# Narrow attention of the third layer: scores on row halves, values as stationary blocks on column strips, outputs divided after the sums

## The reference

```python
B, LQ, D, H, HD, LK = 4, 256, 256, 16, 16, 64
x = layer_norm(hidden_states, ln1_w, ln1_b)
q = (x @ q_w + q_b).reshape(B, LQ, H, HD).transpose(0, 2, 1, 3)
k = (encoder_hidden_states @ k_w + k_b).reshape(B, LK, H, HD).transpose(0, 2, 1, 3)
v = (encoder_hidden_states @ v_w + v_b).reshape(B, LK, H, HD).transpose(0, 2, 1, 3)
scores = jnp.einsum('bhqd,bhkd->bhqk', q, k) / 4
scores = jnp.where(mask, scores, finfo.min)
attn = jax.nn.softmax(scores, axis=-1)
out = jnp.einsum('bhqk,bhkd->bhqd', attn, v).transpose(0, 2, 1, 3).reshape(B, LQ, D)
hidden = out @ cproj_w + cproj_b + residual
```

## Time and profile before

| what | before |
| --- | --- |
| median of 3 runs | 957.06 us |
| lowest, highest | 953.86, 961.48 us |
| span of the profiled execution | 957.6 us |
| PE busy | 881.7 us (92%), 5624 matmul records |
| DVE, ACT, POOL busy | 604.0, 491.8, 484.3 us |
| chain that ended last | PE 70%, DVE 19%, issue 5%, POOL 3% |
| attention 2, first turn to MLP 2's second block | 529.4 to 616.7 us |

### The profile page before, as it was taken

One profiled execution on the slowest core, in us unless ns is written; L12 is line 12 of the kernel. 1 busy time (PEld: TensorE's weight loads), 2 busy tenths in 40 slices (PEclk: granted clock), 3 DMA queues, 4 the chain that ended last, 5 costly groups with the idle time before them and its releaser, 6 DMA issues.

```text
span 957.6 us, 15739 instructions
## 1 busy us (share of the span) xinstructions
PE 881.7 (92%) x5624; PEld 737.2 (77%) x5624; DVE 604.0 (63%) x1344; ACT 491.8 (51%) x1205; POOL 484.3 (51%) x507
## 2 busy tenths in 40 slices
PE   4889876899999999999899898899999999999898
PEld 3677755899966789666797787899975689757788
DVE  3688887416779757796423545325779867798440
ACT  2566655654753356533663332764763347632662
POOL 2667876474543345465293170184544335465383
PEclk8699999999999999999999988999999999999999
DMA  6823312002550025200002000101570015200001
GB/s 188 294 91 87 102 38 96 5 2 72 168 213 1 1 70 162 100 1 0 23 2 88 1 2 0 64 37 40 160 254 0 1 35 164 67 1 1 1 12 34
DMA packets 26673, 64.04 MB, mean 67 GB/s; under 512 B 2995, under 2 KB 15843, under 8 KB 25444
## 3 DMA queue, kind: packets, MB, share of 16 engines
q1 hardware_dynamic: 26596, 63.03, 20.2%
HBM read 57.22 MB, written 5.77 MB: 66 GB/s over the span
## 4 chain that ended last, share of the span: by engine, by line
PE 70%; DVE 19%; issue 5%; POOL 3%; ACT 1%; DMA 1%; SPq 1%; DVEq 0%; POOLq 0%
PE ps L964 7%; PE ps L904 6%; PE ps L863 6%; PE ps L865 6%; PE ps L893 5%; PE ps L940 4%; PE ps L762 3%; PE ps L705 3%; PE ps L706 3%; PE ps L707 3%; PE ps L686 3%; DVE prob L1658 3%; PE ps L687 3%; PE ps L688 3%; DVE mx L1657 3%
## 5 line engine op out<-in xcount | busy, mean ns | idle before, releaser
L964 PE MATMUL ps<-arena,pT_all 128*128 128x256 f32 x512 | 116.6, 381 | 5.7 <-DVE x L1678 3.6
L964 PEld LDWEIGHTS ps<-arena,pT_all 128*128 128x128 f32 x512 | 96.2, 190 | 32.3 <-issue 15.1
L940 PE MATMUL ps<-arena,hT 128*128 128x512 f32 x256 | 115.5, 594 | 0.0
L536 POOL TENSOR_TENSOR rstd<-var,neg_half 128x1 f32<-128x1 f32 (+1 forms) x56 | 33.9, 606 | 155.1 <-DVE var L1487 155.1
L543 POOL TENSOR_TENSOR arena<-arena,rinv 128x640 f32<-128x640 f32 x64 | 80.4, 1257 | 55.4 <-DVE rinv L1472 55.3
L570 POOL TENSOR_TENSOR prob<-prob,rinv 128x512 f32<-128x512 f32 x32 | 49.5, 1547 | 113.2 <-DVE rinv L1671 113.2
L1196 ACT ACTIVATE arena<-ps,nb 128x320 f32<-128x320 f32 x128 | 66.4, 523 | 58.1 <-DVE nb L1458 57.9
L1239 ACT ACTIVATE arena_r<-ps,cols 128x256 fp32r<-128x256 f32 x128 | 66.5, 520 | 55.1 <-PE ps L688 55.0
L512 POOL TENSOR_TENSOR vacc<-vacc,vpart 128x256 f32<-128x256 f32 x60 | 44.0, 734 | 98.6 <-ACT vpart L1311 98.3
L589 POOL TENSOR_TENSOR arena_r<-arena,arena_r 128x512 fp32r<-128x512 f32 x64 | 83.9, 1333 | 13.2 <-ACT arena L1240 13.2
L686 PE MATMUL ps<-hH,w1H 128*128 128x256 f32 x256 | 75.2, 294 | 11.9 <-DVE prob L1658 5.1
(11 more groups left out here) (164 smaller groups left out, 2350.9 us busy)
## 6 DMA issues: line engine op xcount, KB each, us to landing
ring<-in_heads_dram SPq DMA_DIRECT2D x64, 512.5 KB, 3.6
w<-in_w_dram SPq DMA_DIRECT2D x8, 1024.0 KB, 7.3
first_r<-spare_k SPq DMA_DIRECT2D x24, 160.0 KB
first_q<-spare_q SPq DMA_DIRECT2D x48, 64.0 KB, 2.6
spare_k<-HL SPq DMA_DIRECT2D x8, 320.0 KB, 2.4
spare_q<-HL SPq DMA_DIRECT2D x8, 256.0 KB, 2.3
x<-in_x_dram SPq DMA_DIRECT2D x1, 1024.0 KB, 6.0
lnb<-in_lnb_dram SPq DMA_DIRECT2D x4, 256.0 KB, 6.6
```

What stands on the lines that cost most here:

```text
L940: last = mm(ps[:, SCORES[k][half], :], hT[:, k, d, 0:P], A[:, d, b // 2, cols_of, sl, :].rearrange("p r s k -> p r (s k)"), start=(d == 0) ...
L964: last = mm(ps[:, 6, 0:D], pT[:, k, c, :], VW[:, b, c, :], start=(c == 0), stop=(c == PAIRS - 1))
```

## The change

The scores of a group of four heads are now two matmuls, each with half of the rows (64: two heads) and 128 columns, into banks 0 and 1; KC is half as wide. The values are now the stationary side: for each pair of heads a block of 32 columns, on one of four column strips, with the turned probabilities as 128 moving columns; the result comes out turned already, in bank 2. Beside it a constant block of ones (sums_of, set by POOL at the start) on the same strips gives each head's sum on all 16 rows of the head, in the right half of bank 2. The DVE takes the reciprocal of these 128x256 sums and multiplies; its product is what output takes as stationary. So the turns of the outputs, and ACT's copies of them, are gone. The value bias goes into VC by a one-row matmul behind each vc job. Rows and columns of the value and output weights are permuted on the host (_by_strip), so that strips match. The order within the iterations is new on PE, ACT and DVE, and the part of MLP 2 woven into the end uses other banks. The core of the diff (left out: sizes and semaphores that fall away, the constants at the start, ACT's removed helper):

```diff
@@ -159,15 +158,15 @@
-        KC = arena[:, 9728:13824].rearrange("p (m b n) -> p m b n", m=4, b=B)
-        VC = arena[:, 13824:14912].rearrange("p (b r e c) -> p b r e c", b=B, r=PAIRS, e=2)
+        KC = arena[:, 9728:11776].rearrange("p (m b n) -> p m b n", m=4, b=B)
+        VC = arena[:, 11776:12800].rearrange("p (b r e c) -> p b r e c", b=B, r=PAIRS, e=2)
-        bo = sb("bo", [1, 4, D])
+        bo = sb("bo", [1, 5, D])
@@ -212,7 +211,7 @@
         qT2 = arena[:, 4096:5120].rearrange("p (k m n) -> p k m n", k=2, m=4)
-        on = arena[:, 5120:5632].rearrange("p (k n) -> p k n", k=2)
+        inv2 = arena[:, 5120:5376]
         oT = sb("oT", [P, 2, DH, P])
@@ -335,12 +331,12 @@
         def up_slot(l, b, f):
             if b == 0 and l > 0:
-                bank, half = (((2, 4, 5, 6) if l == 2 else (0, 1, 2, 5))[f // 2], f % 2)
+                bank, half = (((0, 4, 5, 6) if l == 2 else (0, 1, 2, 5))[f // 2], f % 2)
             else:
...
-        TURN_M = ((7, 7), (7, 7), (4, 2), (7, 7))
+        TURN_M = ((7, 7), (7, 7), (4, 7), (7, 7))
         SCORES = ((0, 1), (2, 5))
         def turn_bank(l, b):
@@ -591,12 +591,7 @@
                         pool.wait_ge(rows_done, rows_before("M1"))
-                        g.memset(arena[:, 9728:14912], 0.0).then_inc(kc_step, 1)
-                        pool.wait_ge(kc_step, 1)
-                        g.memset(VC[0:C, :, :, 0, HD:VO], 1.0).then_inc(kc_clear, 1)
-                        pool.wait_ge(kc_clear, 1)
-                        g.memset(VC[C:P, :, :, 1, HD:VO], 1.0).then_inc(kc_clear, 1)
-                        pool.wait_ge(kc_clear, 2)
+                        g.memset(arena[:, 9728:12800], 0.0).then_inc(kc_clear, 1)
@@ -655,8 +650,9 @@
                         for d in range(DH):
-                            m = mm(o[:, 0:D], ctxD[:, d, i, :], vw2[:, 0, d, :], start=(d == 0), stop=(d == 1))
-                        m.then_inc(proj_ps, 1)
+                            mm(o[:, 0:D], ctxD[:, d, i, :], vw2[:, 0, d, :], start=(d == 0), stop=False)
+                        mm(o[:, 0:D], ones[0:1, :], bo[:, 4, :], start=False, stop=True).then_inc(proj_ps, 1)
             def turn_m(l, b):
@@ -1019,8 +1015,12 @@
                 def scores(g):
...
                     pe.wait_ge(q_ready, g + 1)
+                    if g >= 1:
+                        pe.wait_ge(s_used, base + g)
                     for m in range(4):
-                        last = mm(ps[:, m, 0:4 * C], qT2[:, k, m, :], KC[:, m, b, :], start=True, stop=True)
+                        for s in range(2):
+                            at = slice(C * s, C * s + C)
+                            last = mm(ps[:, s, m * P:(m + 1) * P], qT2[at, k, m, :], KC[at, m, b, :], start=True, stop=True)
                     last.then_inc(s_ps, 1)
                 def turn_p(g):
@@ -1035,68 +1035,61 @@
                 def values(g):
...
                     pe.wait_ge(pT_act, n + 1)
-                    for r in range(PAIRS):
-                        at = 256 + r % 4 * 2 * VO
-                        last = mm(ps[:, r // 4, at:at + 2 * VO], pT[:, k, r, :],
-                                  VC[:, b, r, :, :].rearrange("p e c -> p (e c)"), start=True, stop=True)
+                    if g >= 1:
+                        pe.wait_ge(oT_ready, g)
+                    for s in range(2):
+                        for w in range(2):
+                            for m in range(4):
+                                c = 4 * s + m
+                                at = slice(32 * m, 32 * m + 32)
+                                what = VC[:, b, c, :, :].rearrange("p e c -> p (e c)") if w == 0 else sums_of[:, :]
+                                last = mm(ps[at, 2, w * D + s * P:w * D + (s + 1) * P], what, pT[:, k, c, :],
+                                          start=True, stop=True)
                     last.then_inc(pv_ps, 1)
                 def output(g):
                     pe.wait_ge(oT_ready, g + 1)
+                    if g >= 1:
+                        pe.wait_ge(rows_done, rows_before("L2") + g)
                     for d in range(DH):
-                        last = mm(ps[:, 3, 256:512], oT[:, g % 2, d, :], vw2[:, 1, d, :], start=(d == 0), stop=(d == 1))
+                        last = mm(ps[:, 3, 0:D], oT[:, g % 2, d, :], vw2[:, 1, d, :], start=(d == 0), stop=(d == 1))
                     last.then_inc(o_ps, 1)
-                def turns(gz, go):
-                    if 1 <= gz <= TILES:
-                        pe.wait_ge(h_ready, base + gz)
-                    if 1 <= go <= TILES:
-                        pe.wait_ge(oT_ready, go)
-                    if 0 <= go < TILES:
-                        pe.wait_ge(on_ready, go + 1)
-                        for d in range(DH):
-                            last = nc.tensor.transpose(ps[:, 7, 256 + d * P:256 + (d + 1) * P],
-                                                       on[:, go % 2, d * P:(d + 1) * P], ident[:, :])
-                        last.then_inc(oT_ps, 1)
-                    if gz < TILES:
-                        pe.wait_ge(z_ready, base + gz + 1)
-                        for d in range(DH):
-                            last = nc.tensor.transpose(ps[:, 7, d * P:(d + 1) * P],
-                                                       z[:, gz % 2, 0, d * P:(d + 1) * P], ident[:, :])
-                        last.then_inc(zT_ps, 1)
-                turns(0, -1)
-                turns(1, -1)
+                def turn_z2(g):
+                    if g >= 1:
+                        pe.wait_ge(h_ready, base + g)
+                    pe.wait_ge(z_ready, base + g + 1)
+                    for d in range(DH):
+                        last = nc.tensor.transpose(ps[:, 7, d * P:(d + 1) * P],
+                                                   z[:, g % 2, 0, d * P:(d + 1) * P], ident[:, :])
+                    last.then_inc(zT_ps, 1)
+                turn_z2(0)
+                turn_z2(1)
                 queries(0)
-                for i in range(TILES + 3):
-                    if 1 <= i <= TILES:
-                        pe.wait_ge(s_used, base + i)
-                    if i >= 3:
-                        pe.wait_ge(on_ready, i - 2)
-                    if i >= 4:
-                        pe.wait_ge(rows_done, rows_before("L2") + i - 3)
-                    if 2 <= i < TILES + 2:
-                        values(i - 2)
-                    if i >= 3:
-                        output(i - 3)
+                for i in range(TILES + 2):
                     if i < TILES:
...
                         queries(i + 1)
+                    if 2 <= i <= TILES:
+                        output(i - 2)
+                    if i + 2 < TILES:
+                        turn_z2(i + 2)
                     if i == TILES - 1:
                         turn_m(2, 0)
-                    elif i == TILES + 1:
-                        pe.wait_ge(hid_ready, 2 * B * FT + 2)
+                    elif i == TILES:
                         turn_m(2, 1)
+                        pe.wait_ge(s_used, base + TILES)
+                        up(2, 0, range(0, 4))
+                    if 1 <= i <= TILES:
+                        values(i - 1)
+                    if i == TILES + 1:
                         up(2, 0, range(4, FT))
-                    if i < TILES + 2:
-                        turns(i + 2, i - 2)
-                    if i == TILES:
-                        up(2, 0, range(0, 4))
+                        output(TILES - 1)
             def mlp(l):
@@ -1140,7 +1133,7 @@
                     at = slice(32 * j, 32 * j + 32)
-                    last = copy(KC[at, i, :, j * C:(j + 1) * C], o[at, 0:B * C].rearrange("p (b n) -> p b n", b=B),
+                    last = copy(KC[at, i, :, j % 2 * C:(j % 2 + 1) * C], o[at, 0:B * C].rearrange("p (b n) -> p b n", b=B),
                                 cols[at, c:c + 1])
@@ -1360,14 +1346,14 @@
             def attend2(seq):
                 base = seq * TILES
-                act.wait_ge(kc_clear, 2)
+                act.wait_ge(kc_clear, 1)
                 for n in range(0, NJ, 2):
...
                 scaled(base + 1, "L2_ln1_w", "L2_ln1_b")
-                for i in range(TILES + 2):
-                    if 1 <= i <= TILES:
+                for i in range(TILES + 1):
+                    if i >= 1:
                         n, k = base + i - 1, (i - 1) % 2
@@ -1379,17 +1365,13 @@
                             .then_inc(e_ready, 1)
-                    if i >= 2:
-                        if i + 2 < TILES:
-                            act.wait_ge(zT_ps, base + i + 3)
-                        turned_o(i - 2, "L2_v_b", 256)
                     if i + 2 < TILES:
...
                     elif i == TILES:
+                        turned_m(2, 1)
                         gelus(2, 0, range(0, 4))
-                        turned_m(2, 1)
                 gelus(2, 0, range(4, FT))
@@ -1717,39 +1699,35 @@
                 def values(g):
-                    k = g % 2
```

(48 more changed lines are left out.)

14 lines of the change are left out of this document (7 added, 7 removed).

## The result

The changed kernel takes 943.73 us (median of 4 runs, 942.92 to 945.42) against 956.66 (4 runs, 953.86 to 961.48): the ratio is 0.9871 with a 95% interval of 0.9838 to 0.9904. It is faster, by 12.9 us or 1.3%; 942 was forecast, with 936 to 951 as the range.

A forecast was written before the change was run, and what follows sets the result against it. The PE-DVE hand-over over shared PSUM banks was taken to set attention 2's period. Terms -2.3, -13.3, -2.05 and +2.5 summed to -15.2 us from 957.6, giving 942.4, forecast as 942, range 936 to 951.

The forecast's parts named there:

- the DVE's ring: Attention 2's loop: all the DVE does for one tile, put at 6.87 us, more than PE's 5.9, so the bound.
- PE's list: Attention 2's loop: all PE has to do for one tile without waits, put at 5.9 us.
- S2 to S7: From scores of tile 2 to scores of tile 7: 46.59 us before, 33.3 after, -13.3.
- X: The DVE's add to x in the loop, 0.33 us; the next scores no longer need it.
- S0 to S2: From scores of tile 0 to scores of tile 2: 11.64 us before, 9.3 after, -2.3.
- Tail: From scores of tile 7 to MLP 2's second block: 24.75 us before, 22.7 after with one clock fall of 1.7, -2.05.
- Projection: Four one-row bias matmuls behind the value jobs, where PE is the bound: 4 x 0.63 = +2.5 us.
- S: PE's scores of one tile: 16 row-half records, two at a time, 0.9 plus 0.2 us for entering and leaving, 1.1.
- V: PE's value matmuls of one tile: 32 records on four overlapping strips, 1.1 us instead of 1.78.
- Rival 4: Part-array matmuls don't overlap in attention 2: PE's list 9.4 us, 963 us in all, slower than before; chance 0.06.
- If only S doesn't overlap: +2: Case within Rival 4: scores alone run serially, hidden behind the DVE's division in all but the first two tiles: +2.
- Rival 1: The clock still falls in attention 2's loop: three falls, +2 to +5 us, about 946; chance 0.17.

The follow-up runs named there:

- e6: Changed kernel with the old matmul forms, small reciprocal and no bias matmul, keeping the new order and the values' own bank: 947.54 us.
- e1: Changed kernel with scores again as 8 full-row records per tile instead of 16 row halves: 943.68 us.
- e2: Changed kernel with a copy of the sums in place of the reciprocal, division left out: 939.50 us.
- e3: Changed kernel with the reciprocal done twice per tile, one behind the other: 961.92 us.
- e8: Changed kernel with the value bias added by the DVE in its copies out of PSUM instead of by one-row matmuls: 936.98 us.
- e9: Changed kernel with both edits, e7's tail order and e8's value bias in the copies: 939.14 us, 0.9806 of the kernel before.
- e4: Changed kernel with the same 32 value records issued strip by strip, all of one strip before the next: 950.75 us.
- e11: Changed kernel with full-row matmuls of zeros in place of the one-row value-bias ones, value bias left out: 939.75 us.
- e7: Changed kernel with another tail order: MLP spreads behind the divisions of tiles 5 and 6, PE's turn behind four up blocks: 943.79 us.
- e12: The changed kernel run once more, unaltered, on the same chip: 943.07 us, 0.9854 of the kernel before.

## Why the prediction was right, step by step

The mechanism was right. The hand-over of PSUM banks between PE and the DVE set the period, with a fall of the clock on top, and the new order frees it of both (e6); then the DVE's ring binds with PE's list just below (e1, e2, e3 move the loop by about what each predicts). The terms of the sum, one by one:

- *S2 to S7, -13.3; measured -15.03.* The reciprocal is the mis-sized term: 1.75 us instead of 2.02. From 16 elements (257 ns) to 256 it costs (1750 - 257) / 240 = 6.2 ns each, not the 7.4 of the step from 2 to 16; why the slope falls, the rows don't say. The Trainium skill's rule (VectorE: DVE Perf Modes, First, the fixed hardware budget), estimated at 2.26 us in the prediction, lies further off; the measurement decides. Five times 0.27 is 1.35 of the 1.7 us; z at 0.32 instead of 0.41, in four tiles, is the rest. (The first of the five periods, taken as 6.3, doesn't follow from its rows: 6.87 less X is 6.54.) PE's list, 5.9, is 6.0.
- *S0 to S2, -2.3; measured -2.17.* Right.
- *Tail, -2.05; measured -3.41.* The fall of the clock that I kept there came (0.78 and 0.88 at 580 to 590), but it hit turns and values, part of them while output would have waited for the DVE, so it cost 0.8 us (e8's tail, at full clock, is 20.56) and not the 1.7 counted; and two shorter reciprocals on the path give 0.5. Order alone had 1.6 us more to give (e9 against e8).
- *Projection, +2.5; measured +3.09, and +1.58 behind it.* The pairs cost 0.62 us each as in the earlier trace rows; the four records of a value job next to them also take 1.06 us instead of 0.93 (3.73 / 4). The fall of the clock ahead of S0 was not foreseen. This step failed: a matmul priced by its own row, with nothing for what it does to its neighbours and for the fall that came with it.
- *Overlap.* S 1.09 and V 1.0 where 1.1 and 1.1 were taken. Rival 4 didn't come; e4 shows that with another order half of it would have: V 2.39. (By its own terms, rival 4's list is 8.9 us and not 9.4: 5.9 less 2.2 and plus 5.2.) "If only S doesn't overlap: +2" is near the +1.63 of e1 by luck: S isn't hidden in the loop, where PE becomes the bound (+1.63), the first two tiles pay 1.51, and the tail got 1.28 back with a full clock.
- *Rival 1.* No fall in the loop: it came just ahead of it, behind the one-row matmuls. Neither of the two things that I saw ahead of each fall in before, gaps and 34-column matmuls, brings it alone: e3 has the gaps and e6 the 34 columns, and the loop's clock is full in both. Both together, as in before, were not tried in another order.

The errors nearly cancelled, so that the sum came this close is luck in part: loop and tail gave 3.1 us more than forecast, the projection and the fall behind it took 2.2 back, and attention 2 gave -15.94 for -15.2. The forecast time has one more slip. The sum was made against the span, 957.6, and the median of the time, 957.06, was taken as the same thing. The time is about 2 us longer than the span (942.92 for 941.1 after; another execution of before with a span of 957.6 took 959.73). So the profiled execution of before lay some 2.7 us above the median. That fits the -2.22 us ahead of attention 2, but no profile of another execution of before shows it; the late fall of the clock took back 1.5.

## What to carry to other kernels

Ask first which hand-over closes the ring, and try the new order and a bank of its own with the old forms: here that was 13.2 of 15.9 us, over half of it in falls of the clock that went with the old order. Once two engines' lists stand within 0.3 us of each other, work taken from one of them is worth only what is left until the other binds; look for it in the stretches where one alone is on the path (the tail here: 1.6 us by order, 2.8 by the reciprocal, at full clock). A bias that came by one-row matmuls at the end of a stage cost 4.7 us here and 0.2 in a copy that has to be made anyway.

## What the runs showed of the hardware that was not expected

- A pair of one-row records costs 0.62 us where a full-row pair costs 0.43 (e11), and four of them behind the value jobs were followed by a granted clock of 0.50, 1.2 GHz, for about 3 us or more in 7 of 7 profiles. In e2, e3 and e7 the slice from 535 to 540 is still at 0.50.
- A reciprocal of 256 elements per row takes 1.75 us, of 16 0.257: 6.2 ns for each further one, where a copy of 256 takes 0.42 us in all (e2).
- Row halves of 64 overlap in pairs: 16 records in 1.09 us, against 1.83 for 8 full ones. Strips overlap only where neighbouring records lie on different strips: 32 records in 1.0 or 2.39 us.
- The clock falls at places that the change doesn't touch: from 879.8 to 882.5 us PE's up blocks start 0.21 us apart instead of 0.12, and behind attention 2 the 14 profiles fall into two sets, 342.35 to 342.98 us (9) and 340.88 to 341.03 (5), that have nothing of the change in common. And in attention 0 before's slices from 20 to 40 us are at 0.50, while after has 0.82 and 0.84 from 30 on; e12, the same kernel as after, has 0.84 and then 0.50. What decides that stays open; such stretches are worth 1.5 to 2 us, as much as a step of this study, so spans alone should not be compared.
